# Interleaving the high and low halves of streamed weights, and spacing the ring they land in

## The chip, the cores and the metric

One core of one Trainium2 chip runs the whole program. The time is device microseconds of one execution. Lower is better.

## The reference

A transformer layer in f32 on x of 4 x 1024 x 512: attention with 16 query heads over 4 key and value heads (three quarters of the keys pooled), a residual and a layer norm, then a feed-forward part with Walsh-Hadamard transforms, another residual and a layer norm. The part that matters here:

```python
x = fwht(x * SU_ug) / SCALE
x_up = x @ W_up.T * (Wscale_ug[:INTER] * SCALE)        # 4096 x 512 by 512 x 2048
x_gate = x @ W_gate.T * (Wscale_ug[INTER:] * SCALE)    # 4096 x 512 by 512 x 2048
x = jax.nn.silu(x_gate) * x_up
x = fwht(x * SU_dp) / SCALE
x = x @ W_down.T * (Wscale_dp * SCALE)
```

## The kernel before

**Split numbers.** Every f32 factor is held as a high part (rounded to the matmul's fp32r type) and a low part (the rest). A product of two factors takes three matmuls: high by high, high by low, low by high.

**Blocks and pairs.** The feed-forward part goes through 8 blocks of 512 tokens (`FBLK`), and in each through 8 pairs of 128-row chunks of the inner dimension (`PAIRS`). Up and gate of a pair are computed together by a scheme of seven products instead of eight (`MULS`, L1880): product k multiplies a sum of weight quarters by a sum of token quarters. A product has 12 matmuls: m (2 output halves of 256 columns) by c (2 contraction chunks) by the three passes. Each has 128 x 128 weights out of `ring` and 256 columns out of `x_hi` or `x_lo`, and a weight load of its own. Results go to the PSUM banks `bank_a`, `bank_b`, `bank_c`, from which ACT (L1549, L1535) and DVE (L1711, L1721, L1723, L1735, L1740) take them. After the products of a pair come the down matmuls of the pair before (L106 to L108): 24 of 512 columns, weights `h_hi` and `h_lo`, columns from `d_hi` and `d_lo`.

**The ring.** There are 56 products' worth of weights (`PRODUCTS`), the same for each block. `ring` has 8 slots (`RING`), one product each: 128 partitions by [part, m, c, 128], 4096 bytes a partition, part 0 the high and part 1 the low halves. Product n is in slot n % 8. In block 0, ACT's `round_product` (L1523) writes the high part of a slot and DVE's `lower_product` (L1660) the low part, out of `raw` and `sums`, five products ahead of the matmuls; SP stores the slot to `gu_dram` (L1323). From then on SP loads each slot again as soon as its product is done (L1332), eight products ahead. The matmuls of block 0 wait for `ring_lo`, those of later blocks for the transfer.

**Where things lie.** The buffers stand in memory in the order in which they are declared: the eight slots, `d_hi` and `d_lo` (4096 bytes each), 64 bytes of room, `x_hi` (14336 bytes, 2048 for each k), `x_lo`. So slot i begins 4096 x (10 - i) + 64 bytes ahead of `x_hi`. The first token chunks of block 0 use slots 5 to 7 for a moment as scratch (`begin_hi`, `begin_lo`).

**Around the products.** In pairs 4 to 6 of each block the next block's tokens are transposed (L1831, four matmuls, plain f32) and transformed (L1839, L1840) between products; in block 0 the down weights are transformed as well (L1851). Each engine follows its own fixed order of instructions, and they meet through semaphores.

Of the kernel before, what the change touches and what calls it, by code (L numbers as in the profile page):

```python
# [19 lines left out]
F32 = mybir.dt.float32  # L20
F32R = mybir.dt.float32r
# [4 lines left out]
P = 128  # L26
# [29 lines left out]
PRODUCTS = PAIRS * MULS  # L56
RING = 8
# [29 lines left out]
def tools(nc, ctx, sems, tag):  # L87

    def sb(name, shape, dt=F32):
        return ctx.enter_context(nc.sbuf_tensor(f"{tag}_{name}", shape, dt))  # L90

    def ps(name, shape):
        return ctx.enter_context(nc.psum_tensor(f"{tag}_{name}", shape, F32))

    def signal(name, per):
        return Signal(sems, nc, f"{tag}_{name}", per)

    def sem(name):
        return sems.enter_context(nc.semaphore(f"{tag}_{name}"))

    return sb, ps, signal, sem
# [1105 lines left out]
def ffn_block(nc, sems, io, x1_dram, mixed_dram, gu_dram, out_dram, held, held_in, last_added):  # L1207
# [3 lines left out]
    with ctx:  # L1211
        sb, ps, signal, sem = tools(nc, ctx, sems, "ff")
# [2 lines left out]
        had, ident, su, sd, dps, ug_scale = (held[n] for n in ("had", "ident", "su", "sd", "dps", "ug_scale"))  # L1215
        raw = [sb(f"raw{i}", [P, 4, 512]) for i in range(2)]
        sums = sb("sums", [P, 3, 512])
        ring = [sb(f"ring{i}", [P, 2, 2, 2, P], F32R) for i in range(RING)]
        d_hi, d_lo = sb("d_hi", [P, 2, D], F32R), sb("d_lo", [P, 2, D], F32R)
        sb("gap_in_front", [P, 16])  # L1220
        x_hi, x_lo = sb("x_hi", [P, MULS, 2, HB2], F32R), sb("x_lo", [P, MULS, 2, HB2], F32R)
        sb("gap_behind", [P, 1008])
        xs_hi, xs_lo = sb("xs_hi", [P, FB], F32R), sb("xs_lo", [P, FB], F32R)
# [67 lines left out]
                    xm[:, 2:4, 0:HB2], by_half(xm[:, 7, :]), xm[:, 2:4, HB2:FB])[k]  # L1291

        def both(slot, part):
            return ring[slot][:, part, :, :, :].rearrange("p m c n -> p (m c n)")


        begin_hi = [xs_hi[:, :], both(5, 0), both(6, 0), both(7, 0)]
        begin_lo = [xs_lo[:, :], both(5, 1), both(6, 1), both(7, 1)]

        MIXED = (7, 10, 9, 11, 8, 12, 8)  # L1300

# [188 lines left out]
        def scalar_program(act):  # L1490
# [22 lines left out]
            def round_product(n):  # L1513

                p, k = divmod(n, MULS)
                if n >= RING:
                    act.wait_ge(*mul_s.now((n - RING) // MULS, (n - RING) % MULS + 1))
                    act.wait_ge(ring_in[n % RING].sem, 16 * (n // RING))
                if k in (0, 4, 5):
                    act.wait_ge(raw_in[p % 2], 16 * (p // 2 + 1))  # L1520
                else:
                    act.wait_ge(sum_s, 4 * p + {1: 2, 2: 1, 3: 3, 6: 4}[k])
                act.activation(both(n % RING, 0), operand(p, k), ACT.Copy).then_inc(ring_hi, 1)  # L1523
# [296 lines left out]
        def tensor_program(pe):  # L1820
# [32 lines left out]
            def multiply(s, blk, p, k, first):  # L1853

                n = MULS * p + k
                r, bank = ring[n % RING], (bank_a, bank_b, bank_c, bank_b, bank_a, bank_b, bank_c)[k]
                if first:
                    pe.wait_ge(ring_lo, n + 1)
                else:
                    pe.wait_ge(*ring_in[n % RING].now(blk - 1, 16 * (n // RING + 1)))  # L1860
                if p == 0:
                    pe.wait_ge(*x_lo_s.now(blk, k + 1))
                if k == 0:
                    pe.wait_ge(*prod_s.last(s, 1))
                elif k == 1:
                    pe.wait_ge(*evict_s.last(s, 4))
                elif k == 2:
                    pe.wait_ge(*evict_s.last(s, 5))
                elif k == 3:
                    pe.wait_ge(*evict_s.now(s, 1))  # L1870
                elif k == 4:
                    pe.wait_ge(*m1_s.now(s, 1))
                elif k == 5:
                    pe.wait_ge(*evict_s.now(s, 2))
                else:
                    pe.wait_ge(*evict_s.now(s, 3))
                for m in range(2):
                    for c in range(2):
                        for a, b in ((0, x_hi), (0, x_lo), (1, x_hi)):
                            i = pe.matmul(bank[:, m, :], r[:, a, m, c, :], b[:, k, c, :], start=(k < 3 and m == 0 and c == 0 and b is x_hi and a == 0),  # L1880
                                          stop=(m == 1 and c == 1 and a == 1), skip_group_check=True)
                i.then_inc(mul_s.sem, 1)

# [15 lines left out]
            def body(blk, idx, parity, first, last):  # L1899
                def at(p, pos):  # L1900
                    folded = 0 if not first else 2 * p + (pos > 1) + (pos > 7)
                    if not last and (p, pos) in X_AT:
                        what, c = X_AT[p, pos]
                        if what == "turn":
                            turn_x(blk + 1, idx + parity, c, 1 - parity, folded)
                        else:
                            mix_x(blk + 1, c, folded)
                    if first and pos in fold_at(p):
                        done = [X_AT[at][0] for at in X_AT if at < (p, pos)]
                        mix_down(2 * p + pos // 7, done.count("turn"), done.count("mix"))  # L1910
                for p in range(PAIRS):
                    s = blk * PAIRS + p
                    for k in range(MULS):
                        multiply(s, blk, p, k, first)
                        at(p, k)
                    if first and p == 0:
                        at(p, 7)
                        continue
                    if p == 1:
                        pe.wait_ge(*added.last(blk, FT))  # L1920
                    down(s - 1, (p - 1) % 2, p == 1, p == 0, False, lambda: at(p, 7))
                    at(p, 8)
                if last:
                    down(blk * PAIRS + PAIRS - 1, 1, False, True, True)
# [23 lines left out]
def layer_kernel(nc, io, out):  # L1948
    x1_dram = nc.dram_tensor("x1_scratch", [B * T, D], F32, kind="Internal").ap()
    mixed_dram = nc.dram_tensor("mixed_scratch", [WP, P, IC, WC], F32, kind="Internal").ap()  # L1950
    gu_dram = nc.dram_tensor("gu_scratch", [PRODUCTS, P, 2, 2, 2, P], F32, kind="Internal").ap()
    io["x"] = io["x"].rearrange("b (t p) d -> b t p d", p=P)
    sems = ExitStack()
    with sems:
        ctx = ExitStack()
        with ctx:
            held, _, _, sem = tools(nc, ctx, sems, "h")
            kept = {"ident": held("ident", [P, P]), "had": held("had", [P, P]), "su": held("su", [P, DC]), "sd": held("sd", [P, IC]),
                    "dps": held("dps", [P, D]), "ug_scale": held("ug_scale", [P, 2, IC]), "y0": held("y0", [P, FT, D])}
            held_in = [sem("held_in"), sem("first_in")]  # L1960
            blocks = x1_dram.rearrange("(n t p) d -> n p t d", t=FT, p=P)
            at = attention_block(nc, sems, io, x1_dram.rearrange("(b t p) d -> b t p d", t=TILES, p=P), mixed_dram, blocks[0], kept, held_in)
            ff = ffn_block(nc, sems, io, blocks, mixed_dram, gu_dram, out.rearrange("b (m t p) d -> (b m) p t d", t=FT, p=P), kept, held_in,
                           at.added.now(B - 1, TILES))
            with nc.Block() as block:

                @block.sync
                def _(sp):
                    ahead = ff.sync(sp)
                    ahead.run(at.sync(sp, ahead))  # L1970

                @block.gpsimd
                def _(pool):
                    ahead = ff.gpsimd(pool)
                    ahead.run(at.gpsimd(pool, ahead))

                @block.scalar
                def _(act):
                    ahead = ff.scalar(act)
                    ahead.run(at.scalar(act, ahead))  # L1980

                @block.vector
                def _(dve):
                    ahead = ff.vector(dve)
                    ahead.run(at.vector(dve, ahead))

                @block.tensor
                def _(pe):
                    ahead = ff.tensor(pe)
                    at.tensor(pe, ahead)  # L1990
                    ahead.run()
# [62 lines left out]
```

## Time and profile before

| | us |
|---|---|
| median of 3 runs | 1590.44 (1589.4 to 1592.46) |
| the profiled execution | 1588.98 |
| its span, first to last instruction | 1587.2 |
| PE busy | 1536.2 (97%), 10280 matmuls |
| DVE busy | 1040.3 (66%) |
| ACT busy | 615.9 (39%) |
| POOL busy | 465.3 (29%) |
| mean granted TensorE clock | 0.995 |

A matmul's time in a row runs from its start to its modelled end and overlaps the next one's, so the pace of a series is read from the distance of the starts. The kernel has some 530 us of attention, then block 0 up to about 677 us, then seven equal blocks of about 127 us, and an end of 25 us.

### The profile page before, as it was taken

The page shows a single profiled execution, that of the slowest core. Times are in us where ns is not written, and L with a number is a line of the kernel's source. Part 1 is how long each engine was busy: PE and PEld are TensorE (multiplying, and loading weights), DVE is VectorE, ACT ScalarE, POOL GpSimd, SP SyncE. Part 2 cuts the span into 40 slices and gives each one's busy share as a digit, 9 for nine tenths or more (in the row PEclk, how much of TensorE's full clock was granted, in tenths as well). Part 3 has the DMA queues.
Part 4 walks back from the last instruction along what each step waited for, and adds up shares of the span by engine and source line. Part 5 has one row for each costly group of instructions (what it writes and reads, how often), then busy time and mean ns, then how long its engine had stood idle before and what let it go on. Part 6 is the DMA issues. An engine that isn't in the chain of part 4 may idle for free.

```text
span 1587.2 us, 26579 instructions
## 1 busy us (share of the span) xinstructions
PE 1536.2 (97%) x10280; PEld 1384.1 (87%) x10280; DVE 1040.3 (66%) x1771; ACT 615.9 (39%) x1257; POOL 465.3 (29%) x584
## 2 busy tenths in 40 slices
PE   6999999999998899999999999999999999999997
PEld 5987988888887788899999999999999999999996
DVE  6866776677677888875575576566566457557544
ACT  4253245235226544433333343343343333333322
POOL 5465456447338533500120030030030030012001
PEclk9999999999999999999999999999999999999998
DMA  7031122122222687588668677767766866866771
GB/s 271 4 123 54 34 89 92 34 81 100 70 80 81 265 320 263 205 300 292 225 225 293 222 242 253 265 219 265 266 232 227 290 221 244 291 226 224 268 247 46
DMA packets 92060, 307.44 MB, mean 194 GB/s; under 512 B 9888, under 2 KB 10272, under 8 KB 90144
## 3 DMA queue, kind: packets, MB, share of 16 engines
q1 hardware_dynamic: 90928, 301.54, 54.0%
q10 hardware_dynamic: 1008, 4.20, 0.7%
q8 instruction: 83, 1.36, 0.3%
q14 instruction: 41, 0.34, 0.1%
HBM read 255.37 MB, written 50.33 MB: 193 GB/s over the span
## 4 chain that ended last, share of the span: by engine, by line
PE 88%; DVE 7%; ACT 2%; issue 1%; DMA 1%; ACTq 0%; POOL 0%; DVEq 0%; POOLq 0%
PE ff_bank_b L1880 16%; PE ff_bank_a L1880 11%; PE ff_bank_c L1880 11%; PE ff_acc L106 7%; PE ff_acc L108 7%; PE ff_acc L107 7%; PE at_big L106 2%; PE at_big L108 2%; PE at_big L107 2%; PE at_mid L1092 2%; PE at_big L1009 2%; PE at_acc L106 2%; PE at_acc L108 2%; PE at_big L999 2%; PE at_acc L107 2%; DVE ff_d_lo L1670 1%
## 5 line engine op out<-in xcount | busy, mean ns | idle before, releaser
L1880 PE MATMUL ff_bank_b<-ff_x_hi,ff_ring 128*128 128x256 f32 x1536 | 304.5, 281 | 10.5 <-DVE ff_x_lo L1655 3.7
L1880 PEld LDWEIGHTS ff_bank_b<-ff_x_hi,ff_ring 128*128 128x128 f32 x1536 | 249.2, 189 | 12.9 <-issue 7.6
L1880 PE MATMUL ff_bank_b<-ff_x_lo,ff_ring 128*128 128x256 f32 x768 | 215.2, 280 | 0.0
L106 PE MATMUL ff_acc<-ff_d_hi,ff_h_hi 128*128 128x512 f32 x512 | 204.6, 400 | 2.7 <-DVE ff_d_lo L1670 2.7
L1880 PE MATMUL ff_bank_c<-ff_x_hi,ff_ring 128*128 128x256 f32 x1024 | 204.7, 283 | 0.0
L1880 PE MATMUL ff_bank_a<-ff_x_hi,ff_ring 128*128 128x256 f32 x1024 | 204.0, 282 | 0.0
L108 PE MATMUL ff_acc<-ff_d_hi,ff_h_lo 128*128 128x512 f32 x512 | 200.2, 391 | 0.0
L107 PE MATMUL ff_acc<-ff_d_lo,ff_h_hi 128*128 128x512 f32 x512 | 200.0, 391 | 0.0
L1880 PEld LDWEIGHTS ff_bank_a<-ff_x_hi,ff_ring 128*128 128x128 f32 x1024 | 165.9, 188 | 2.7 <-issue 0.2
L1880 PEld LDWEIGHTS ff_bank_c<-ff_x_hi,ff_ring 128*128 128x128 f32 x1024 | 165.9, 189 | 1.9 <-issue 1.9
L1711 DVE TENSOR_TENSOR ff_c<-ff_bank_b,ff_c 128x512 f32<-128x512 f32 x64 | 44.2, 691 | 163.9 <-PE ff_bank_b L1880 163.9
L1880 PEld LDWEIGHTS ff_bank_b<-ff_x_lo,ff_ring 128*128 128x128 f32 x768 | 144.6, 188 | 0.0
L1880 PE MATMUL ff_bank_a<-ff_x_lo,ff_ring 128*128 128x256 f32 x512 | 143.2, 280 | 0.0
L1880 PE MATMUL ff_bank_c<-ff_x_lo,ff_ring 128*128 128x256 f32 x512 | 143.2, 280 | 0.0
L1535 ACT ACTIVATE ff_sg<-ff_c,h_ug_scale 128x512 f32<-128x512 f32 (+1 forms) x128 | 79.0, 617 | 140.8 <-DVE ff_c L1735 106.3
L106 PEld LDWEIGHTS ff_acc<-ff_d_hi,ff_h_hi 128*128 128x128 f32 x512 | 96.5, 189 | 23.0 <-issue 4.7
L1549 ACT ACTIVATE ff_c<-ff_bank_a 128x512 f32<-128x512 f32 x64 | 38.3, 599 | 200.2 <-PE ff_bank_a L1880 199.2
L1755 DVE TENSOR_TENSOR ff_h_lo<-ff_hf,ff_h_hi 128x512 fp32r<-128x512 f32 x128 | 103.7, 847 | 18.0 <-ACT ff_h_hi L1587 17.4
L108 PEld LDWEIGHTS ff_acc<-ff_d_hi,ff_h_lo 128*128 128x128 f32 x512 | 96.5, 189 | 21.4
L107 PEld LDWEIGHTS ff_acc<-ff_d_lo,ff_h_hi 128*128 128x128 f32 x512 | 96.6, 189 | 20.1 <-issue 1.7
L1419 POOL TENSOR_TENSOR ff_xm<-ff_xm 128x512 f32<-128x512 f32 x7 | 9.0, 1292 | 310.7 <-ACT ff_xm L1505 310.7
L1880 PEld LDWEIGHTS ff_bank_a<-ff_x_lo,ff_ring 128*128 128x128 f32 x512 | 96.3, 188 | 2.7 <-issue 0.2
(306 smaller groups left out, 3508.6 us busy)
## 6 DMA issues: line engine op xcount, KB each, us to landing
ff_ring<-gu_scratch SPq DMA_DIRECT2D x392, 512.0 KB, 4.9
gu_scratch<-ff_ring SPq DMA_DIRECT2D x56, 512.0 KB, 4.9
at_xt<-in_xt SPq DMA_DIRECT2D x4, 2048.0 KB, 8.4
at_xn<-in_x SPq DMA_DIRECT2D x32, 256.0 KB, 3.1
x_scratch<-at_x SPq DMA_DIRECT2D x32, 256.0 KB, 2.0
ff_raw<-in_wgu SPq DMA_DIRECT2D x8, 1024.0 KB, 6.8
at_wd_a<-in_wd SPq DMA_DIRECT2D x8, 512.0 KB, 4.0
mixed_scratch<-at_wd_a SPq DMA_DIRECT2D x8, 512.0 KB, 3.9
```

What stands on the lines that cost most here:

```text
L106: pe.matmul(out, lhs_hi, rhs_hi, start=first, stop=False)
L107: pe.matmul(out, lhs_hi, rhs_lo, start=False, stop=False)
L108: return pe.matmul(out, lhs_lo, rhs_hi, start=False, stop=last)
L999: i = pe.matmul(qf[:, P * t:P * t + P], xt[:, c, P * t:P * t + P], wkv[:, c, 0:128], start=(c == 0), stop=(c == DC - 1))
L1009: i = pe.matmul(big[:, 2 + t, :], xt[:, c, REMOTE + P * t:REMOTE + P * t + P], wkv[:, c, :], start=(c == 0), stop=(c == DC - 1))
L1092: plain = lambda c: pe.matmul(mid[:, 0, 0:H * NB], xt[:, c, P * t:P * t + P], m_sb[:, c, :], start=(c == 0), stop=(c == DC - 1))
L1535: return act.activation(target, source, ACT.Silu, scale=ug_scale[:, 1, 2 * p + j:2 * p + j + 1])
L1549: act.activation(c2[:, 0, :, :], bank_a[:, :, :], ACT.Copy).then_inc(m1_s.sem, 1)
L1670: i = dve.tensor_tensor(by_piece(d_lo[:, j, :]), down_chunk(2 * p + j), by_piece(d_hi[:, j, :]).bitcast(F32), ALU.subtract)
L1711: dve.tensor_tensor(c12[:, :, :], bank_b[:, :, :], c2[:, 0, :, :], ALU.add).then_inc(evict_s.sem, 1)
L1755: dve.tensor_tensor(h_lo[q][:, 1 - j, :], hf[:, 1 - j, :], h_hi[q][:, 1 - j, :].bitcast(F32), ALU.subtract).then_inc(h_lo_s.sem, 1)
L1880: i = pe.matmul(bank[:, m, :], r[:, a, m, c, :], b[:, k, c, :], start=(k < 3 and m == 0 and c == 0 and b is x_hi and a == 0), stop=(m == 1 ...
```

## The change

The ring's slots get another inner order: [m, c, 128, part] instead of [part, m, c, 128], so that the high and the low half of one weight stand side by side. A matmul's weights are then 128 elements with a step of two elements (8 bytes). ACT and DVE write their half with the same step. The scratch uses of slots 5 to 7 take contiguous halves of a slot, as before. `gu_dram` gets the same order, so the transfers stay contiguous. Between two slots stand 128 bytes (`ring_gap`), none behind the last.

```diff
-        ring = [sb(f"ring{i}", [P, 2, 2, 2, P], F32R) for i in range(RING)]
+        def staggered(i):
+            slot = sb(f"ring{i}", [P, 2, 2, P, 2], F32R)
+            if i < RING - 1:
+                sb(f"ring_gap{i}", [P, 32])
+            return slot
+
+        ring = [staggered(i) for i in range(RING)]
...
         def both(slot, part):
-            return ring[slot][:, part, :, :, :].rearrange("p m c n -> p (m c n)")
-
-
-        begin_hi = [xs_hi[:, :], both(5, 0), both(6, 0), both(7, 0)]
-        begin_lo = [xs_lo[:, :], both(5, 1), both(6, 1), both(7, 1)]
+            return ring[slot][:, :, :, :, part].rearrange("p m c n -> p (m c n)")
+
+        def half(slot, part):
+            return ring[slot][:, part, :, :, :].rearrange("p c n a -> p (c n a)")
+
+        begin_hi = [xs_hi[:, :], half(5, 0), half(6, 0), half(7, 0)]
+        begin_lo = [xs_lo[:, :], half(5, 1), half(6, 1), half(7, 1)]
...
-                            i = pe.matmul(bank[:, m, :], r[:, a, m, c, :], b[:, k, c, :], start=(k < 3 and m == 0 and c == 0 and b is x_hi and a == 0),
+                            i = pe.matmul(bank[:, m, :], r[:, m, c, :, a], b[:, k, c, :], start=(k < 3 and m == 0 and c == 0 and b is x_hi and a == 0),
...
-    gu_dram = nc.dram_tensor("gu_scratch", [PRODUCTS, P, 2, 2, 2, P], F32, kind="Internal").ap()
+    gu_dram = nc.dram_tensor("gu_scratch", [PRODUCTS, P, 2, 2, P, 2], F32, kind="Internal").ap()
```

## Rows read from the trace of the kernel before

**Rows 1.** The page: busy times, and the chain that ended last by line.

```profile
PE 1536.2 (97%) x10280; PEld 1384.1 (87%) x10280; DVE 1040.3 (66%) x1771; ACT 615.9 (39%) x1257; POOL 465.3 (29%) x584
PE 88%; DVE 7%; ACT 2%; issue 1%; DMA 1%; ACTq 0%; POOL 0%; DVEq 0%; POOLq 0%
PE ff_bank_b L1880 16%; PE ff_bank_a L1880 11%; PE ff_bank_c L1880 11%; PE ff_acc L106 7%; PE ff_acc L108 7%; PE ff_acc L107 7%; PE at_big L106 2%; PE at_big L108 2%; PE at_big L107 2%; PE at_mid L1092 2%; PE at_big L1009 2%; PE at_acc L106 2%; PE at_acc L108 2%; PE at_big L999 2%; PE at_acc L107 2%; DVE ff_d_lo L1670 1%
```

**Rows 2.** Windows of block 0 and block 1: length, busy (instructions), clock, DMA.

```profile
533.00:677.00 144.00, 133.97 (x876) 118.75 (x875) 126.71 (x170) 70.77 (x129) 64.00 (x50) 0.98 0.72 271
683.00:805.00 122.00, 121.69 (x868) 114.27 (x867) 70.84 (x111) 42.94 (x76) 18.52 (x16) 1.00 0.74 262
```

**Rows 3.** Waits of PE in blocks 1 to 7: total us, times, longest.

```profile
PE ff_bank_b L1880 <- DVE ff_c L1721: 1.9, 6, 0.3
```

**Rows 4.** Timeline of PE, block 2: start, us, merged count; the products' first matmuls.

```profile
905.09 0.28 PE L1880 MATMUL ff_bank_a<-ff_x_hi,ff_ring 128*128 128x256 f32 x1
...
906.51 0.28 PE L1880 MATMUL ff_bank_b<-ff_x_hi,ff_ring 128*128 128x256 f32 x1
...
907.92 0.28 PE L1880 MATMUL ff_bank_c<-ff_x_hi,ff_ring 128*128 128x256 f32 x1
...
909.34 0.28 PE L1880 MATMUL ff_bank_b<-ff_x_hi,ff_ring 128*128 128x256 f32 x1
```

**Rows 5.** Timeline of PE, pair 6 of blocks 1 and 6: second matmuls of products.

```profile
784.36 0.28 PE L1880 MATMUL ff_bank_a<-ff_x_lo,ff_ring 128*128 128x256 f32 x1
...
787.08 0.28 PE L1880 MATMUL ff_bank_c<-ff_x_lo,ff_ring 128*128 128x256 f32 x1
...
1419.03 0.28 PE L1880 MATMUL ff_bank_a<-ff_x_lo,ff_ring 128*128 128x256 f32 x1
...
1421.75 0.28 PE L1880 MATMUL ff_bank_c<-ff_x_lo,ff_ring 128*128 128x256 f32 x1
```

**Rows 6.** Timeline of PE in block 0, behind a wait (in brackets).

```profile
540.36 0.35 PE L1880 MATMUL ff_bank_b<-ff_x_hi,ff_ring 128*128 128x256 f32 x1 [1.78 <-DVE ff_x_lo L1655]
540.56 0.28 PE L1880 MATMUL ff_bank_b<-ff_x_lo,ff_ring 128*128 128x256 f32 x1
...
541.92 0.28 PE L1880 MATMUL ff_bank_a<-ff_x_lo,ff_ring 128*128 128x256 f32 x1
```

**Rows 7.** Timeline of PE in block 0, granted clock at its half level.

```profile
562.06 0.41 PE L1880 MATMUL ff_bank_b<-ff_x_lo,ff_ring 128*128 128x256 f32 x1
...
562.91 0.41 PE L1880 MATMUL ff_bank_a<-ff_x_hi,ff_ring 128*128 128x256 f32 x1
```

**Rows 8.** Timeline of PE in the attention: 13 plain f32 matmuls, last lasts 592 ns.

```profile
21.69 5.74 PE L1009 MATMUL at_big<-at_wkv,at_xt 128*128 128x512 f32 x13
L1009 PE MATMUL at_big<-at_wkv,at_xt x64: 592/592/595, 20.4 to 401.9; 128*128 128x512 f32 x64
```

**Rows 9.** Timeline of PE, down matmuls of block 2.

```profile
899.64 0.39 PE L108 MATMUL ff_acc<-ff_d_hi,ff_h_lo 128*128 128x512 f32 x1
...
903.73 0.39 PE L108 MATMUL ff_acc<-ff_d_hi,ff_h_lo 128*128 128x512 f32 x1
```

**Rows 10.** Timeline of weight loads: four of the transposes, and the next load.

```profile
783.70 0.46 PEld L1831 LDWEIGHTS ff_x_ps<-h_ident,h_y 128*128 128x128 f32 x4
784.13 0.19 PEld L1880 LDWEIGHTS ff_bank_a<-ff_x_hi,ff_ring 128*128 128x128 f32 x1
```

**Rows 11.** The ring's writers: shortest, median and longest ns, first and last start.

```profile
L1660 DVE TENSOR_TENSOR ff_ring<-ff_raw,ff_ring x32: 674/688/1776, 501.2 to 667.0; 128x512 fp32r<-128x512 f32 x32
L1523 ACT ACTIVATE ff_ring<-ff_raw x32: 613/618/667, 500.5 to 666.4; 128x512 fp32r<-128x512 f32 x32
```

**Rows 12.** Groups of DVE from 600 to 1550 us, shapes apart: busy, mean ns.

```profile
L1675 DVE SCALAR_TENSOR_TENSOR ff_hf<-ff_c,h_ug_scale,ff_sg 128x512 f32<-128x512 f32 x60 | 45.0, 749 | 0.0
L1723 DVE TENSOR_TENSOR ff_c<-ff_bank_c,ff_c 128x512 f32<-128x512 f32 x59 | 40.8, 691 | 2.0
L1675 DVE SCALAR_TENSOR_TENSOR ff_hf<-ff_c,h_ug_scale,ff_sg 128x256 f32<-128x256 f32 x60 | 30.0, 499 | 0.0
```

**Rows 13.** The page's DMA issues: count, KB each, median us to landing.

```profile
ff_ring<-gu_scratch SPq DMA_DIRECT2D x392, 512.0 KB, 4.9
gu_scratch<-ff_ring SPq DMA_DIRECT2D x56, 512.0 KB, 4.9
```

## The prediction

> **What bounds the kernel now.** I read four views, in this order. The page's busy shares and its chain [rows 1]: PE is busy for 1536.2 of 1587.2 us, 88% of the chain is PE, and the seven products alone hold 38% of it (16 + 11 + 11), all at one line. The windows by block [rows 2]: a later block has PE busy for 121.69 of 122.00 us at full clock, DVE for 70.84 and ACT for 42.94; only block 0, which also makes the ring's contents, has PE idle (10 of 144 us) with DVE at 126.71. The waits of PE in blocks 1 to 7 [rows 3]: 1.9 us in all. So from 683 us on nothing but the rate of the matmuls sets the time, and what a weight load or a matmul costs is paid in full.
>
> That rate stands in the timeline, not in the durations (a row's 0.28 us overlaps its neighbours). Twelve matmuls make a product; from the first of bank_a at 905.09 to the first of the fourth product at 909.34 are 36 matmuls in 4.25 us, 118.1 ns each, one load to each matmul [rows 4]. The same instructions also run faster: from 784.36 to 787.08 are 24 steps in 2.72 us, 113.3 ns each, in products 4 to 6 of pair 6 of block 1, right after four transposes, and at the same place in each block up to the sixth (1419.03 to 1421.75, the same 2.72) [rows 5]. In block 0 a wait of 1.78 us is followed by such a stretch in other ring slots (540.56 to 541.92 are 12 steps in 1.36 us) [rows 6]. Operands, shapes and distances are alike, so a part of the pitch depends on how the load and the moving stream meet in time. They are 18 products of the 392 of blocks 1 to 7 (three in each of six blocks; the first block's and the last's stand in the rows) and 6 in block 0.
>
> **What the pitch is made of.** At the full level of the granted clock, 2.4 GHz, 256 columns need 106.7 ns. Block 0 has a stretch at the half level: 562.06 to 562.91 are four steps, 213 ns each, which is 256 columns at 1.2 GHz with nothing on top [rows 7]. At full clock there are 11.4 ns on top (118.1 - 106.7), or 6.6 in the fast stretch. Plain f32 matmuls of 512 columns take (5.74 - 0.592)/12 = 429 ns, 2.3 ns above 512 columns at 1.2 columns a ns, with a load each too [rows 8]. Down's 512 columns take 227 ns (899.64 to 903.73 are 18 steps), 14 above 213.3 [rows 9]. And loads of 128 columns follow each other at 0.43/4 = 108 ns in the transposes [rows 10]: the load isn't the longer of the two. Hence the extra exists only where the moving stream runs at 2.4 columns a ns, twice the pace of the load. In both cheap cases both walk through memory at the same pace, 4 bytes a step each.
>
> **The interleaving, main term.** The load's 128 elements now lie 8 bytes apart, 1024 bytes in all, like the 1024 bytes of the 256 moving columns beside it. In about 107 ns both walk over equal distances: the pace is equal again, at full clock. If the extra comes from the two streams meeting again and again as one overtakes the other, it meets at most once now. The trace has no strided weight load, so I bound the new pitch from the rows: 108 (loads alone, by the transposes' rows), 118.1 if nothing changes, and above it the next part's rival. I take 113.4, the one value below 118.1 that these very instructions show. Sum: (392 - 18) x 12 x (118.1 - 113.4 = 4.7 ns; by the long averages of the two stretches 4.4) = 19.8 us with 4.4. Block 0: 48 products that are neither fast nor at half clock, x 12 x 4.4 ns = 2.5 us, of which I take half, 1.3, since waits stand there. In the last pair of blocks 1 to 6 PE waits for DVE's L1721 behind product 4 [rows 3]; five products that end earlier by 53 ns each lengthen that wait by up to 0.26 us, six times 1.6 us, and I take half, -0.8. That is 20.3 us.
>
> A rule speaks for no effect at all. The trace shows one load beside each matmul and 11.4 ns above the columns' own time [rows 4]. The Trainium skill, "TensorE: Matmul & The Clock Gate", section "Step-by-step: what each phase is for", says that PE has two independent read ports and that loading the next weights takes no read bandwidth from the running matmul. By that rule the extra isn't the load's doing, the stride changes nothing, and the main term is 0; it is a rival below.
>
> **The gaps.** 128 bytes behind each of the first seven slots. Slot 7 keeps its distance to x_hi (d_hi, d_lo and 64 bytes between), slot i is 128 x (7 - i) bytes further off. Before, all slots had the same place relative to x within 4096 bytes, and all ran at 118 whichever slot it was, so no row says what another distance does. In lockstep a bad distance would stay bad through a load; a good one stays good. I take 0 and keep one bad slot of eight in the range: 672 matmuls x 9 ns = 6 us. Everything behind the ring moves by 896 bytes together; only hr against xs and ident against y1 lie on either side of it, in some hundred matmuls: nothing.
>
> **Writing the ring.** In block 0 and just ahead of it ACT writes 56 high halves (median 618 ns) and DVE reads and writes 56 low ones (median 688) [rows 11], now with 8 bytes between elements. Below zero is excluded, since no element less is moved. Above, the price of doing every element twice: 512 x (749 - 499)/256 = 0.50 us on DVE by the 512 and the 256 column form of L1675 [rows 12], x 51 in block 0 = 25.5 us, of which 17 fit into the time in which DVE is idle there (144 - 126.71) [rows 2]; so up to 8.5, with ACT's share 10 us. I take 0, the end that today's 688 ns is nearer to: L1723, which moves as many elements by another pattern, is at 691 [rows 12]. The first four token chunks of block 0 use slots 5 to 7 as contiguous scratch as before, 512 floats each: 0.
>
> **The transfers.** 56 stores and 392 loads of the ring keep 4096 contiguous bytes a partition at both ends: 512 KB, 4.9 us to landing [rows 13]. A slot is asked for when its product ends and is needed seven products later, 7 x 1.36 = 9.5 us even at the faster pitch, and the down products (5.4 us a pair) come on top, so landing stays hidden. If that cover were gone, each product would wait; the DMA share of 0.74 [rows 2] rises to 0.75.
>
> **Rivals.** (a) Nothing changes: the extra belongs to the matmul at full clock and not to how the load reads. For it: all slots, both x halves and also other weights show 118, and the rule above. Against it: the two pitches for the same work [rows 4, 5]. 1590.4 us. (b) Slower: a load now touches twice as much memory per element, so it takes twice as many turns from the moving stream. Place: every one of the 5376 matmuls; price: the 9 ns by which 11.4 exceeds the 2.3 of the plain f32 case [rows 4, 8], once more, x 4704 matmuls of blocks 1 to 7 = 42.3, plus half of block 0 = 3; 1590.4 + 45 = 1636 us. It decides from the point at which the strided load's turns are more than lockstep saves; for it speaks that the stream already has nothing to spare at full clock; against it that at equal pace the rows show almost none. Its far end: a load that needs twice its 108 ns would be the longer of the two, pitch 220, +550 us; nothing in the rows bears that out. On that, the Trainium skill, "Advanced Engine Details and Errata", section "SBUF Cachelines", says that a 16-byte line must be hit at least twice for full rate; a step of 8 bytes hits it exactly twice, so by the page the load keeps its rate, and at the very edge. No row here shows a strided load. (c) Mixed: some distances gain, others lose; with half of the slots at 113.4 and half 4 ns above 118 it is again 1590, and anything between (forecast) and (b).
>
> **How the numbers follow.** The profiled execution took 1588.98 us (span 1587.2, 1.8 around it), the median is 1590.44, 1.46 above it. 1588.98 - 20.3 = 1568.7, and + 1.46 = 1570.1: predicted 1570. Chances: a gain like the forecast's or larger 0.37, a smaller gain out of (c) 0.06; no change, (a) and the middle of (c), 0.23; slower, (b) with the bad side of (c) and the ring's writes, 0.34, of which 0.08 lies above 1645. A change of 0.2%, 3.2 us, is about what can be told from none. The forecast's own range is 1556 (pitch 111) to 1582. The range that should hold the time takes in (a), (b) and the ring's 10 us: 1556 to 1645.
>
> **What would show it.** Right: in a block's timeline 36 matmuls take 4.08 us instead of 4.25, in all slots; a block of 121.35 us becomes about 118.6; down's 227 stays; L1660 and its ACT partner stay at 688 and 618 ns; PE's waits for L1721 grow a little. Wrong: a pitch of 118 everywhere (a), above 124 (b), or one that goes with the slot (c); a DVE line in block 0 near 1 us would show the strided writes.

## The result, and the profile after

The changed kernel takes 1603.51 us (median of 4 runs, 1601.04 to 1606.28) where the kernel before takes 1591.34. The two medians are 12.2 us apart; the ratio of the times is 1.0089, with a 95% interval of 1.0074 to 1.0103. (Here and below the ratio isn't the quotient of the medians printed beside it, and can differ from it by some 0.1%.) It is slower by 0.8 to 0.9%, 12 to 14 us. The forecast was 1570, a gain.

The page of the changed kernel: busy times, the chain's share by engine, two groups of the products (the line is now L1888) and the ring's transfers.

```profile
PE 1552.1 (97%) x10280; PEld 1399.6 (87%) x10280; DVE 1040.3 (65%) x1771; ACT 618.3 (39%) x1257; POOL 466.2 (29%) x584
PE 88%; DVE 7%; ACT 3%; issue 1%; DMA 1%; ACTq 0%; DVEq 0%; POOL 0%; POOLq 0%
L1888 PE MATMUL ff_bank_b<-ff_x_hi,ff_ring 128*128 128x256 f32 x1536 | 310.2, 284 | 9.6 <-DVE ff_c L1719 3.4
L1888 PEld LDWEIGHTS ff_bank_b<-ff_x_hi,ff_ring 128*128 128x128 f32 x1536 | 259.4, 197 | 12.1 <-issue 6.8
ff_ring<-gu_scratch SPq DMA_DIRECT2D x392, 512.0 KB, 4.9
```

PE is busy for 15.9 us more than in [rows 1]; DVE and the transfers are as they were, and ACT is busy for 2.4 us more. The timeline of PE in block 3 gives the new pace (first matmuls of four successive products, start and length in us):

```profile
944.20 0.28 PE L1888 MATMUL ff_bank_a<-ff_x_hi,ff_ring 128*128 128x256 f32 x1
...
945.64 0.28 PE L1888 MATMUL ff_bank_b<-ff_x_hi,ff_ring 128*128 128x256 f32 x1
...
947.09 0.28 PE L1888 MATMUL ff_bank_c<-ff_x_hi,ff_ring 128*128 128x256 f32 x1
...
948.52 0.28 PE L1888 MATMUL ff_bank_b<-ff_x_hi,ff_ring 128*128 128x256 f32 x1
```

36 steps in 4.32 us, 120.0 ns each, where [rows 4] had 118.1. From all starts inside the products of blocks 1 to 7 (each product's first interval left out) the mean is 120.26 ns, against 117.58 before, or 117.8 without the 18 fast products. The faster stretches of [rows 5] are gone: none of the 392 products is below 119.5 ns. And a weight load's own row has grown from a median of 188 to 198 ns (before, then after):

```profile
L1880 PEld LDWEIGHTS ff_bank_b<-ff_x_hi,ff_ring x1536: 186/188/335, 535.2 to 1560.7; 128*128 128x128 f32 x192
L1888 PEld LDWEIGHTS ff_bank_b<-ff_x_hi,ff_ring x1536: 193/198/330, 535.8 to 1575.6; 128*128 128x128 f32 x192
```

Where the 14.8 us between the two spans (1602.0 and 1587.2) arise, by the starts of the blocks' first products: attention 0.5, block 0 3.4, blocks 1 to 7 11.0 (889.99 against 878.99 us from the first product of block 1 to the last of block 7). 2.68 ns by 4704 matmuls would be 12.6 in the last; a net 1.6 came back, and the 1.9 us of waits for DVE's L1721 of [rows 3] are gone (no wait of PE is left in those blocks). In block 0, 48 products at 2.4 ns more are 1.4 us. Most of the other 2 lie at its end, where the granted clock now falls to its half level: the last two products take 147 and 213 ns a matmul, 1.4 us more. Before, the clock was full there. It falls there in `x_gap` below as well, whose weights are contiguous, so this part needn't come from the interleaving (after, then `x_gap`):

```profile
677.00:681.00 4.00, 4.00 (x22) 3.98 (x21) 2.19 (x5) 1.76 (x3) 0.00 (x0) 0.57 0.96 312
674.00:678.00 4.00, 3.40 (x17) 3.43 (x18) 2.79 (x6) 0.67 (x2) 0.99 (x1) 0.60 0.79 244
```

The writers of the ring, the line numbers shifted, beside [rows 11]: DVE 688 to 694 ns, ACT 618 to 662.

```profile
L1668 DVE TENSOR_TENSOR ff_ring<-ff_raw,ff_ring x32: 677/694/1777, 501.7 to 668.7; 128x512 fp32r<-128x512 f32 x32
L1531 ACT ACTIVATE ff_ring<-ff_raw x32: 648/662/713, 501.0 to 667.7; 128x512 fp32r<-128x512 f32 x32
```

### The profile page after: what moved, and what is told of

It is laid out like the page before. It is cut to its first block, busy times and chain, and to the rows that moved or that the text cites. A ratio compares the mean times of both kernels' runs of the same rounds, so it can differ in the third digit from the quotient of the medians.

```text
span 1602.0 us, 26579 instructions
## 1 busy us (share of the span) xinstructions
PE 1552.1 (97%) x10280; PEld 1399.6 (87%) x10280; DVE 1040.3 (65%) x1771; ACT 618.3 (39%) x1257; POOL 466.2 (29%) x584
## 3 DMA queue, kind: packets, MB, share of 16 engines
q8 instruction: 83, 1.36, 0.3%
## 4 chain that ended last, share of the span: by engine, by line
PE 88%; DVE 7%; ACT 3%; issue 1%; DMA 1%; ACTq 0%; DVEq 0%; POOL 0%; POOLq 0%
PE ff_bank_b L1888 16%; PE ff_bank_c L1888 11%; PE ff_bank_a L1888 11%; PE ff_acc L106 7%; PE ff_acc L108 7%; PE ff_acc L107 7%; PE at_big L106 2%; PE at_big L108 2%; PE at_big L107 2%; PE at_mid L1092 2%; PE at_big L1009 2%; PE at_acc L106 2%; PE at_big L999 2%; PE at_acc L108 2%; PE at_acc L107 2%
## 5 line engine op out<-in xcount | busy, mean ns | idle before, releaser
L1888 PE MATMUL ff_bank_b<-ff_x_hi,ff_ring 128*128 128x256 f32 x1536 | 310.2, 284 | 9.6 <-DVE ff_c L1719 3.4
L1888 PEld LDWEIGHTS ff_bank_b<-ff_x_hi,ff_ring 128*128 128x128 f32 x1536 | 259.4, 197 | 12.1 <-issue 6.8
L1888 PE MATMUL ff_bank_b<-ff_x_lo,ff_ring 128*128 128x256 f32 x768 | 217.9, 284 | 0.0
L1888 PE MATMUL ff_bank_c<-ff_x_hi,ff_ring 128*128 128x256 f32 x1024 | 210.0, 287 | 0.0
L1888 PE MATMUL ff_bank_a<-ff_x_hi,ff_ring 128*128 128x256 f32 x1024 | 208.3, 286 | 0.0
L1888 PEld LDWEIGHTS ff_bank_c<-ff_x_hi,ff_ring 128*128 128x128 f32 x1024 | 174.4, 199 | 1.9 <-issue 1.9
L1888 PEld LDWEIGHTS ff_bank_a<-ff_x_hi,ff_ring 128*128 128x128 f32 x1024 | 172.8, 197 | 2.8 <-issue 0.2
L1888 PEld LDWEIGHTS ff_bank_b<-ff_x_lo,ff_ring 128*128 128x128 f32 x768 | 151.8, 198 | 0.0
L1888 PE MATMUL ff_bank_c<-ff_x_lo,ff_ring 128*128 128x256 f32 x512 | 146.0, 285 | 0.0
L1888 PE MATMUL ff_bank_a<-ff_x_lo,ff_ring 128*128 128x256 f32 x512 | 145.2, 284 | 0.0
L1888 PEld LDWEIGHTS ff_bank_c<-ff_x_lo,ff_ring 128*128 128x128 f32 x512 | 102.0, 199 | 1.6 <-issue 1.6
L1888 PEld LDWEIGHTS ff_bank_a<-ff_x_lo,ff_ring 128*128 128x128 f32 x512 | 101.1, 197 | 2.5 <-issue 0.2
```

The source lines that it names most:

```text
L1888: i = pe.matmul(bank[:, m, :], r[:, m, c, :, a], b[:, k, c, :], start=(k < 3 and m == 0 and c == 0 and b is x_hi and a == 0), stop=(m == 1 ...
```

## The experiments

In all of them "pace" is the mean distance of the starts inside the products of blocks 1 to 7, without each product's first interval, into which a wait can fall. A product counts as fast when its mean is below 115 ns. "Distance" is the distance in bytes from a slot to x_hi; only what is left of it modulo 1024 is given. In profiles the attention part ends between 533 and 537 us from run to run, so I compare paces and medians, not single spans.

### The two parts apart

The change without the room between the slots (`il_nogap`):

```diff
-            if i < RING - 1:
-                sb(f"ring_gap{i}", [P, 32])
```

> Interleaved weights, no room between the slots, so every slot has the same distance to x as in the kernel before. Theory I (the step of 8 bytes alone costs the time): same as the changed kernel, pitch 120.2 ns per matmul of 256 columns, about +13 us against the kernel before. Theory D (the differing distances of the gaps cost it): pitch at or below 117.7 ns and a time at or below that of the kernel before.

Measured: 1602.87 us, ratio 1.0079 (1.0063 to 1.0094), pace 120.08 ns. The interleaving alone makes the whole loss, within the intervals.

The kernel before with the room alone (`gap_only`):

```diff
+            if i < RING - 1:
+                sb(f"ring_gap{i}", [P, 32])
```

> Contiguous weights as before, but with the 128 bytes between the slots. Theory I: as the kernel before, pitch 117.7 ns, within 3 us of 1591. Theory D: 120 ns and about +13 us, or a pitch that differs from slot to slot.

Measured: 1575.27 us, ratio 0.9902 (0.9885 to 0.9918), pace 114.54 ns. Neither theory had that: the half of the change that I took as nothing is worth 15 us by itself. Timeline of its block 3, pair 1, the first matmuls of the first four products:

```profile
950.66 0.28 PE L1886 MATMUL ff_bank_a<-ff_x_hi,ff_ring 128*128 128x256 f32 x1
...
952.08 0.28 PE L1886 MATMUL ff_bank_b<-ff_x_hi,ff_ring 128*128 128x256 f32 x1
...
953.44 0.28 PE L1886 MATMUL ff_bank_c<-ff_x_hi,ff_ring 128*128 128x256 f32 x1
...
954.80 0.28 PE L1886 MATMUL ff_bank_b<-ff_x_hi,ff_ring 128*128 128x256 f32 x1
```

The first product takes 1.42 us, 118 ns a matmul. The second takes 1.36, 113.3 ns, and so do all the others of the pair. The pace of [rows 5], which before stood in 18 of 392 products, stands here in 290. In the changed kernel, with the same room, it stands in none.

### Is the strided load itself longer?

Both kernels with each matmul of 256 columns split in two of 128, each with its own load (`half_contiguous`, `half_interleaved`). 128 columns need 53 ns, so it is the loads that set the pace:

```diff
-                            i = pe.matmul(bank[:, m, :], r[:, a, m, c, :], b[:, k, c, :], ...
+                            for w in (slice(0, P), slice(P, 2 * P)):
+                                i = pe.matmul(bank[:, m, w], r[:, a, m, c, :], b[:, k, c, w], ...
```

> The kernel before with each matmul of 256 columns split into two of 128 columns, each with its own weight load, so 10752 loads and matmuls: 128 columns need only 53 ns, and the load sets the distance of the starts. It measures what a contiguous load takes by itself. All theories: 109 to 112 ns from start to start.

> The changed kernel with the same split. Theory L (a load with a step of 8 bytes is itself longer, by the 10 ns that its rows grew, 188 to 198, and the chain of loads sets the 120 ns): start to start about 8 to 10 ns above the contiguous split, 118 to 122 ns. Theory S (the load keeps its length but takes more turns from the moving stream beside it, which here has slack): the same 109 to 112 ns as the contiguous split.

Timelines of the two, first rows of successive products of 24 matmuls (contiguous, then interleaved):

```profile
1139.82 0.39 PE L1881 MATMUL ff_bank_b<-ff_x_hi,ff_ring 128*128 128x128 f32 x2
...
1150.54 0.39 PE L1881 MATMUL ff_bank_b<-ff_x_hi,ff_ring 128*128 128x128 f32 x2
```

```profile
1166.20 0.40 PE L1889 MATMUL ff_bank_b<-ff_x_hi,ff_ring 128*128 128x128 f32 x2
...
1177.64 0.40 PE L1889 MATMUL ff_bank_b<-ff_x_hi,ff_ring 128*128 128x128 f32 x2
```

96 steps each: 10.72 us is 111.7 ns, 11.44 us is 119.2. Over all products it is 111.67 and 118.91, and the kernels took 2142.14 and 2216.36 us (one run each). The second has the room between the slots and the first hasn't. Slot 7 has the same distance in both, and there a product of 24 takes 2.68 and 2.84 us:

```profile
1188.31 0.39 PE L1881 MATMUL ff_bank_b<-ff_x_hi,ff_ring 128*128 128x128 f32 x2
...
1190.99 0.28 PE L1881 MATMUL ff_bank_c<-ff_x_hi,ff_ring 128*128 128x128 f32 x1
```

```profile
1217.11 0.40 PE L1889 MATMUL ff_bank_b<-ff_x_hi,ff_ring 128*128 128x128 f32 x2
...
1219.95 0.28 PE L1889 MATMUL ff_bank_c<-ff_x_hi,ff_ring 128*128 128x128 f32 x1
```

A load of the same 128 x 128 weights takes 7.2 ns longer when its elements are 8 bytes apart, 6.6 at the same distance. Theory L holds. With it, 118.9 of the changed kernel's 120.3 ns are the load's: it has become the bound. What isn't shown is that the load needs this by itself. The interleaved pace goes with the slot (118.3 ns in odd slots, 119.4 to 119.6 in even ones; contiguous 111.7 in all), so the 128 columns beside the load may have a share in it. No run has loads without columns.

Weights with a step of 16 bytes, the halves of both chunks side by side (`step16`):

```diff
-        ring = [sb(f"ring{i}", [P, 2, 2, 2, P], F32R) for i in range(RING)]
+        ring = [sb(f"ring{i}", [P, 2, P, 2, 2], F32R) for i in range(RING)]
...
-                            i = pe.matmul(bank[:, m, :], r[:, a, m, c, :], b[:, k, c, :], ...
+                            i = pe.matmul(bank[:, m, :], r[:, m, :, c, a], b[:, k, c, :], ...
```

> Weights of a product with a step of 16 bytes (both halves of both chunks side by side), no gaps. Theory L (the load is longer by the memory that it walks over: 111.7 ns for 512 bytes, 118.9 for 1024): another 14 ns for 2048 bytes, pace about 133 to 135 ns, about +75 us. Rival E (each element that opens new memory costs a step of its own): a load of twice its length, pace above 200 ns, over +400 us.

```profile
1015.02 0.40 PE L1885 MATMUL ff_bank_b<-ff_x_hi,ff_ring 128*128 128x256 f32 x1
...
1017.82 0.40 PE L1885 MATMUL ff_bank_c<-ff_x_hi,ff_ring 128*128 128x256 f32 x1
```

12 steps in 2.80 us, 233.3 ns, 2186.05 us in all (one run). The length doesn't follow the memory walked over (L would have given 133 to 135): it is 111.7, 118.9 and 233.3 ns for steps of 4, 8 and 16 bytes. The growth is small up to 8 bytes, and at 16 the time is 2.1 times that of contiguous weights, as if each element cost a second turn (rival E). In that run ACT's writes take 1132 ns (median) and DVE's 1114; their patterns also have one dimension more, so the step alone isn't shown to be the reason.

### Does the strided load also take from the stream?

512 moving columns beside each load, so that the stream is the longer (`wide_contiguous`, `wide_interleaved`; both chunks of x go into both halves of the bank, so what they compute isn't the layer):

```diff
-                            i = pe.matmul(bank[:, m, :], r[:, a, m, c, :], b[:, k, c, :], ...
+                            i = pe.matmul(bank[:, :, :], r[:, a, m, c, :], b[:, k, :, :], ...
```

> The kernel before with 512 moving columns beside each weight load of a product instead of 256 (both chunks of x at once, into both halves of the bank), so what it computes is no longer the layer: it measures the pace where the stream, not the load, is the longer. All theories: about 227 ns from start to start, as the down matmuls.

> The changed kernel with the same 512 columns (also no longer the layer). Theory L (the strided load is longer by 7 ns and nothing else is lost): it hides beside 213 ns of stream, so the pace is that of the contiguous one within 1 ns. Theory S (the strided load takes more turns from the stream): the pace is 5 to 9 ns above the contiguous one.

Timelines, 36 steps each (contiguous, then interleaved):

```profile
1021.66 0.39 PE L1880 MATMUL ff_bank_b<-ff_x_hi,ff_ring 128*128 128x512 f32 x1
...
1029.90 0.39 PE L1880 MATMUL ff_bank_a<-ff_x_hi,ff_ring 128*128 128x512 f32 x1
```

```profile
1027.99 0.39 PE L1888 MATMUL ff_bank_b<-ff_x_hi,ff_ring 128*128 128x512 f32 x1
...
1036.32 0.40 PE L1888 MATMUL ff_bank_a<-ff_x_hi,ff_ring 128*128 128x512 f32 x1
```

8.24 us is 228.9 ns, 8.33 is 231.4; over all products 228.84 and 231.87 (one run each, 2170.92 and 2186.38 us). So there is a part of theory S too. On average it is 3 ns, but it goes with the slot: 230.2 to 230.6 ns in even slots, 233.3 to 233.4 in odd ones. Again only the interleaved kernel has the room between the slots. At the same distance, in slot 7, a product of 12 takes 2.75 us with contiguous weights and 2.80 with interleaved ones:

```profile
1198.39 0.39 PE L1880 MATMUL ff_bank_b<-ff_x_hi,ff_ring 128*128 128x512 f32 x1
...
1201.14 0.39 PE L1880 MATMUL ff_bank_c<-ff_x_hi,ff_ring 128*128 128x512 f32 x1
```

```profile
1206.17 0.40 PE L1888 MATMUL ff_bank_b<-ff_x_hi,ff_ring 128*128 128x512 f32 x1
...
1208.97 0.39 PE L1888 MATMUL ff_bank_c<-ff_x_hi,ff_ring 128*128 128x512 f32 x1
```

Over all products of slot 7 it is 228.9 and 233.4 ns: the step by itself costs the stream 4.4 ns there, just under the 5 to 9 that theory S asked for. How much of it remains at 256 columns, where the load is the bound, these runs don't tell.

### What in the ring's room makes the faster pace?

128 bytes between x_hi and x_lo, alone (`x_gap`) and together with the ring's room of 128 bytes (`both_gaps`):

```diff
-        x_hi, x_lo = sb("x_hi", [P, MULS, 2, HB2], F32R), sb("x_lo", [P, MULS, 2, HB2], F32R)
+        x_hi = sb("x_hi", [P, MULS, 2, HB2], F32R)
+        sb("gap_between", [P, 32])
+        x_lo = sb("x_lo", [P, MULS, 2, HB2], F32R)
```

> Kernel before with one gap of 128 bytes between x_hi and x_lo and none in the ring: within each product the moving operand's place relative to the weights jumps by 128 bytes from matmul to matmul (high, low, high). Theory F (the series has two stable paces, 117.7 and 113.3 ns, and a jump of the distance from one matmul to the next makes it fall into the faster, where it stays): nearly all products at 113.3, about 1570 us. Rival G (what counts is the distance itself, as some slots of the spaced ring have it): a fixed pace for x_hi and another for x_lo, or 117.7 for all and 1590 us.

> Kernel before with 128 bytes between the ring's slots and 128 bytes between x_hi and x_lo. Theory F: no slower than either alone, about 1570 us. Rival G: the jumps of both cancel for some slots and the pace depends on the slot.

Measured: for `x_gap` 1595.34 us, ratio 1.0036 (1.0024 to 1.0048), pace 117.30 ns; for `both_gaps` 1594.02 us, 1.0029 (1.002 to 1.0039), 117.78 ns; in neither a product below 115. Theory F falls: jumps inside a product don't lead into the faster pace, and with them it is gone where the ring's room had made it. That both are slower than before at an equal pace has another cause, which I had not watched. The gap also moved h against d, the operands of the down matmuls (timeline of `x_gap`, 15 steps):

```profile
950.38 0.39 PE L106 MATMUL ff_acc<-ff_d_hi,ff_h_hi 128*128 128x512 f32 x1
...
953.87 0.39 PE L106 MATMUL ff_acc<-ff_d_hi,ff_h_hi 128*128 128x512 f32 x1
```

233 ns instead of the 227 of [rows 9]; over all of them in blocks 1 to 7 the mean is 232.9 against 228.4, which by 1536 matmuls is 7 us. From `kgap_64` on the runs keep that distance modulo 1024.

32 bytes instead of 128 between the slots (`scan_contiguous`):

> Kernel before with 32 bytes instead of 128 between the slots, so that slot 7 keeps its distance to x and the others are 32, 64, ... 224 bytes further off. Theory F: jumps of 32 bytes at each product's start; if a jump of any size will do, a pace of 113.3 from the second or third product of a pair on, as with 128 bytes. Rival G: a pace by slot that repeats with the distance, whichever pair it is.

Measured: 1592.76 us (one run), and paces by slot, from slot 7 (distance 64) in steps of 32 to slot 0 (distance 288): 117.0, 119.7, 119.4, 117.9, 117.1, 118.5, 119.1, 117.3 ns. Only 16 products are fast, and all of them lie in slots 7 and 3, which owe their low means to them: without these both are at 117.8 ns, the slow pace of the kernel before. The lowest slow pace is then that of slot 0, 117.3; the distances of 96, 128, 224 and 256 bytes have 118.5 to 119.7. Rival G holds as far as there is a level for each distance. The distance of 64 in the kernel before is at one of the better ones, and the levels are within 2.5 ns of each other; none of them is the 113.3 of the faster pace.

128 bytes behind each k of x, with the ring as before, and x_hi 64 or 192 bytes off (`kgap_64`, `kgap_192`):

```diff
+        wide_hi = sb("x_hi", [P, MULS, 2 * HB2 + 32], F32R)
+        sb("gap_between", [P, 32])
+        wide_lo = sb("x_lo", [P, MULS, 2 * HB2 + 32], F32R)
+        x_hi, x_lo = (t[:, :, 0:2 * HB2].rearrange("p k (c n) -> p k c n", c=2) for t in (wide_hi, wide_lo))
```

> Kernel before with the ring as it was and 128 bytes behind each k of x_hi and x_lo (x_hi begins 64 bytes off the slots' place as before; the distance between down's operands unchanged). In the run with the spaced ring the pace fell to 113.3 ns at boundaries that lead from an odd to an even slot, where the distance of x to the weights goes from 64 to 192 modulo 256, and stayed there. Theory P (that boundary is the trigger): here it is the one from k 0 to k 1 in every pair, so k 0 at 118, k 1 to 6 at 113.3, some 336 of 392 products fast, about 1573 us, 2 us below the spaced ring. Rival Q (the flips came from something else about the ring): 117.7 ns and 1590 us.

> The same with x_hi beginning 192 bytes off instead of 64, so that the boundary from 64 to 192 modulo 256 is the one from k 1 to k 2. Theory P: k 0 and k 1 at 118, k 2 to 6 at 113.3, about 1577 us. Rival Q: no such shift by one product.

Measured: 1589.58 us, ratio 1.0007 (0.9998 to 1.0017), pace 117.75, and 1586.89 (one run), 117.52. Theory P falls: it wanted some 336 fast products, and there are 13 and 28, where the kernel before has 18. The same jump from 64 to 192 bytes, made by x instead of by the weights, mostly shortens only the first interval behind it, to 114 or 115 ns. In 12 places of `kgap_64`, all in pair 5, one whole product is fast, and the next is slow again.

The room between the slots made 256 and 384 bytes, and with 128 bytes x moved by 128 (`gap_256`, `gap_384`, `gap_front`):

```diff
-                sb(f"ring_gap{i}", [P, 32])
+                sb(f"ring_gap{i}", [P, 64])
...
-        sb("gap_in_front", [P, 16])
+        sb("gap_in_front", [P, 48])
```

> Contiguous weights, 256 bytes of room between the slots instead of 128 (the room behind x is cut so that down's operands keep their distance modulo 1024). If only the distance modulo 256 matters, slots are alike again: 117.7 ns in nearly all products and 1590 us. If any spacing of the ring will do: 113.3 ns in some 290 of 392 products and 1575 us.

> The same with 384 bytes, which is 128 modulo 256. Modulo 256: as the ring spaced by 128, flips to 113.3 ns at boundaries from an odd to an even slot, 1575 us. If the period is longer (512 or 1024), other boundaries and another count of fast products, 1575 to 1590 us.

> Contiguous weights, 128 bytes between the slots, and x_hi and x_lo moved by 128 bytes, so that odd and even slots change roles modulo 256. If the flip hangs on the distance (64 before, 192 behind), it moves to boundaries from an even to an odd slot, and the time stays near 1575 us; if it hangs on the slots' own addresses, it stays where it was.

| room between slots, bytes | median us | ratio (interval) | pace, ns | fast products |
|---|---|---|---|---|
| none (kernel before) | 1588.86 | 1 | 117.58 | 18 |
| 128 | 1575.27 | 0.9902 (0.9885 to 0.9918) | 114.54 | 290 |
| 256 | 1589.44 | 1.0002 (0.999 to 1.0014) | 117.55 | 21 |
| 384 | 1574.52 | 0.9912 (0.9889 to 0.9936) | 114.52 | 292 |
| 128, x moved by 128 | 1575.78 | 0.9915 (0.9896 to 0.9933) | 115.03 | 248 |

The second row is `gap_only`, from an earlier series in which the kernel before was at 1590.38 us. The pair of the timeline of `gap_only` again, in `gap_256` and then in `gap_384`:

```profile
955.20 0.28 PE L1886 MATMUL ff_bank_a<-ff_x_hi,ff_ring 128*128 128x256 f32 x1
...
958.03 0.28 PE L1886 MATMUL ff_bank_c<-ff_x_hi,ff_ring 128*128 128x256 f32 x1
...
959.44 0.28 PE L1886 MATMUL ff_bank_b<-ff_x_hi,ff_ring 128*128 128x256 f32 x1
```

```profile
947.98 0.28 PE L1886 MATMUL ff_bank_a<-ff_x_hi,ff_ring 128*128 128x256 f32 x1
...
950.75 0.28 PE L1886 MATMUL ff_bank_c<-ff_x_hi,ff_ring 128*128 128x256 f32 x1
...
952.11 0.28 PE L1886 MATMUL ff_bank_b<-ff_x_hi,ff_ring 128*128 128x256 f32 x1
```

The third product takes 1.41 us in the one and 1.36 in the other. Of 0, 128, 256 and 384 bytes, 0 and 256 act alike and so do 128 and 384, as if only the distance modulo 256 mattered. Look at the boundaries where two products meet without other matmuls between them and the first is slow. In `gap_only` the next product is fast at 59 of the 62 from an odd to an even slot (distance 64 to 192 modulo 256), and at none of 31 from an even to an odd one. Six more changes happen inside a product, product 4 of pair 4. `gap_384` has the same 59 and six. In `gap_front`, where the slots have changed roles, the next product is fast at 60 of 88 boundaries from an even to an odd slot, again from 64 to 192, and at none of 50 of the other kind. This pair has it there from the third product on:

```profile
949.35 0.28 PE L1886 MATMUL ff_bank_a<-ff_x_hi,ff_ring 128*128 128x256 f32 x1
...
952.18 0.28 PE L1886 MATMUL ff_bank_c<-ff_x_hi,ff_ring 128*128 128x256 f32 x1
...
953.54 0.28 PE L1886 MATMUL ff_bank_b<-ff_x_hi,ff_ring 128*128 128x256 f32 x1
```

It hangs on the distance between weights and moving columns, then, and not on the slots' own addresses. The jump isn't enough by itself: of the 28 boundaries of `gap_front` without the change, 22 lie behind a pair's first product.

## Why the prediction was wrong

**The bound.** Right: PE's pace from 683 us on sets the time, and nothing off PE moved it. All but some 2 to 3 us of the loss is that pace.

**The main term.** This step failed: "I bound the new pitch from the rows: 108 (loads alone ...), 118.1 if nothing changes", and the 113.4 taken between them. I priced what the load does to the stream and left the load's own length as it was; measured was 120.3. Two things were off in that:

- The lower bound, and "the load isn't the longer of the two", came from loads beside another kind of matmul. The transposes' loads follow at 108 ns [rows 10], but loads of the products' weights set 111.7 (`half_contiguous`), which is more than the 106.7 of 256 columns. And by [rows 8] 128 plain f32 columns themselves need 107 ns, so the row of the transposes couldn't tell what a load takes.
- With a step of 8 bytes it is 118.9 (`half_interleaved`), 118.3 in the best slots. No pace below that was to be had, and that is above the 117.8 of the slow pace before.

What the pace has on top of the load's did shrink as the step said: 117.8 - 111.7 = 6.1 ns at the slow pace before (1.6 at the fast one), 120.26 - 118.91 = 1.35 after. But the load grew by 7.2. That equal pace through memory is what took the rest away isn't shown; a load that has become the bound would leave little to see of it either way, and beside 512 columns the strided load cost the stream 3 ns more on average, and 4.4 at the same distance, not less.

**The gaps.** Failed as well: "I take 0". With contiguous weights they are worth -15 us, three quarters of what I had expected of the interleaving, and by the very pace that [rows 5] showed. I had written that this pace depends on how load and stream meet in time and had the two layouts' distances at hand, but looked only for a bad slot. Under the interleaving, whose loads allow no pace below some 118 ns, nothing of the gain is left: with the room 1.0089, without it 1.0079, intervals that overlap.

**Writing the ring.** Zero was nearly right: 6 ns on DVE, 44 on ACT (51 x 44 ns = 2 us on an engine that is idle for half of block 0).

**The transfers.** Right: 4.9 us to landing, and no wait of PE for them.

**The wait for L1721.** Right in its mechanism, with the sign turned: slower products removed it. With the faster pace of `gap_only` it grew from 1.9 to 3.0 us:

```profile
PE ff_bank_b L1886 <- DVE ff_c L1727: 3.0, 6, 0.5
```

**Rival (b)** had the sign, 45 us where 13 came. Its mechanism, the stream robbed by the load, is there with 3 to 4.4 ns beside 512 columns; what decided was the length of the load, which (b) had only as a far end of 550 us. The far end exists at twice the stride: `step16`.

**The two rules.** The Trainium skill, "Advanced Engine Details and Errata", section "SBUF Cachelines", asks for two hits on a line of 16 bytes for full rate. The step of 8 bytes, exactly two hits, took 118.9 ns against 111.7, so nearly but not quite full rate; one hit took 233.3. With this measured price of two hits the change would have been forecast slower. The Trainium skill, "TensorE: Matmul & The Clock Gate", section "Step-by-step: what each phase is for", has the load taking no read bandwidth from the running matmul. Here the mean pace changes by 3.0 ns with nothing but the place of the weights (117.58 to 114.54, `gap_only`), and beside 512 columns, where the stream is the longer, by 4.4 ns with nothing but the load's step (slot 7), so the measurement decides against it for these operands.

**Still open:** why the jump from 64 to 192 bytes sets off the faster pace when the weights make it and hardly when x does; why the faster pace ends where other matmuls stand between two products (61 of its 64 ends in `gap_only`); and whether the strided load is longer by itself or loses time to the columns beside it.

**The better version.** The kernel before with 128 bytes between the ring's slots and nothing else beats both: 1575.27 us, 0.9902 of the kernel before.

## What to carry to other kernels

Where each matmul has its own weight load and 256 columns, as here, load and stream are nearly equally long (111.7 and 106.7 ns), and either one's few ns are paid thousands of times. So measure the load with fewer columns beside it before changing how it reads, and keep weights contiguous unless that shows otherwise. When two kernels are compared, compare slots with the same distance between the operands. Then vary the distance between the two operands in steps of 32 to 128 bytes and read the distances between starts, since a layout that costs nothing moved this kernel by 1%. When an edit has two parts, run each alone: here one was worth -15 us and the other hid it.

## What the runs showed of the hardware

- A load of 128 x 128 fp32r weights sets a pace of 111.7 ns with elements 4 bytes apart and 118.9 with 8 (both beside 128 columns), and 233.3 with 16 (beside 256).
- Beside 512 columns, whose stream is the longer, loads with a step of 8 bytes make the pace 233.4 ns instead of 228.9 at the same distance (slot 7).
- The same series of loads and matmuls of 256 columns has two stable paces, 117.8 and 113.3 ns. Which one it is in depends on how it got there: with room of 128 or 384 bytes between slots some three quarters of the products are at the faster, with 256 it is 21 of 392, and with 128 bytes between x_hi and x_lo none.
- Down's matmuls of 512 columns went from a mean of 228.4 to 232.9 ns when their two operands were moved by 128 bytes against each other.
- ACT writes 512 elements in 662 ns with a step of 8 bytes instead of 618, DVE in 694 instead of 688. With 16 bytes and a pattern of one dimension more it is 1132 and 1114.
